# Second expert stage of a two-layer transformer kernel: gates on the inner values, sums kept in PSUM, output matmuls one chunk later

## The chip, the cores and the metric

The kernel runs on one core of a Trainium2 chip. A core has five engines that run on their own and meet through semaphores: TensorE (PE, matmuls), VectorE (DVE), ScalarE (ACT), GpSimd (POOL) and SyncE (SP, which here only issues transfers). PSUM has eight banks of 128 x 512 fp32 values; TensorE writes there, VectorE and ScalarE read. The metric is the device time of one execution in microseconds (us); lower is better.

## The reference, cut to what matters

Two layers, each an attention-like part and an expert part, on 8 x 256 tokens of width 128. Only the expert part of the second layer concerns the change:

```python
def _L1_ffn_ref(hidden_states, Wg, W1, W3, W2):
    B, S, D, F, E, K = (4, 256, 128, 256, 8, 2)
    x = hidden_states.reshape(-1, d)
    gates = jax.nn.softmax(x @ Wg, axis=-1)
    top_g, top_i = jax.lax.top_k(gates, K)
    top_g = top_g / top_g.sum(axis=-1, keepdims=True)
    w = jnp.zeros((t, e), x.dtype).at[jnp.arange(t)[:, None], top_i].add(top_g)
    gate_h = jax.nn.silu(jnp.einsum('td,edf->etf', x, W1))
    up = jnp.einsum('td,edf->etf', x, W3)
    y = jnp.einsum('etf,efd->etd', gate_h * up, W2)
    out = jnp.einsum('te,etd->td', w, y)
    ...
    x = x + gb * _L1_ffn_ref(h, ...)
```

All eight experts are computed for all tokens; the gate w is zero for six of the eight. Since w depends on token and expert alone, it may multiply y or the inner values gate_h * up: the sum is the same but for rounding.

## The kernel before, in words

Everything is held transposed: 128 channels on the partitions, the 2048 tokens along the free axis, in four blocks of 512. The second expert stage goes through 32 steps m = 4 e + t (expert e, token block t). Each step has two chunks c of 128 inner values.

Matmuls are made nearly exact in fp32 by splitting both sides into an upper part (fp32r) and the rest: `three` issues three matmuls, upper by upper, lower weights by upper, upper by lower values. In the profile these are L1055, L1056 and L1057.

For chunk c of step m:

- `hidden1(m, c)` on TensorE: six matmuls into banks c and 2 + c (the W1 and the W3 product), weights from WH and WL, values from HH and HL. It waits until the same chunk of step m - 1 has been read by ScalarE (`act`) and VectorE (`prod`).
- silu on ScalarE, bank c to SG (L587).
- product on VectorE, bank 2 + c times SG, into G (L1025).
- copy on ScalarE, G to its upper part GH (L591).
- subtraction on VectorE, G - GH into GL (L1032).
- `output1(m, c)` on TensorE: three matmuls from GH and GL into bank 4 + t; the two chunks are summed there.

After both chunks `moe_scale` on VectorE (L702) multiplies the bank by the gates WB of the expert and block into YW, and GpSimd adds YW to ACC in SBUF (L297). It is done two steps behind. At the end `residual_acc` (L634) adds ACC, scaled, to X, and SyncE stores X.

TensorE issues `hidden1(m + 1, 0)`, `output1(m, 0)`, `hidden1(m + 1, 1)`, `output1(m, 1)`. The order on each engine is as written; there is no planner. Steps 8 to 23 of TensorE, 8 to 31 of ScalarE are rolled into loops of eight.

Weights: SyncE loads expert e into WS (L224), and GpSimd splits it into WH and WL (L274, L277), in one of two slots. Gates: the routing result CT is stored to memory (L217) and read back, one row spread over all 128 partitions, into one of two slots of WB (L220 for experts 0 and 1, L226 for the rest). L226 waits for `ymul`, the count of finished gate multiplications, and L224 stands behind it in SyncE's queue.

## Time and profile before

| | |
|---|---|
| median of 3 runs | 723.02 us (719.28, 723.02, 723.96) |
| profiled execution | 722.03 us, span 720.2 us |
| TensorE busy | 626.7 us (87%) |
| VectorE busy | 557.3 us (77%) |
| ScalarE busy | 481.3 us (67%) |
| GpSimd busy | 241.2 us (33%) |
| granted TensorE clock, mean | 0.934 |

The span goes from the first to the last instruction on the chip. Busy shares are means over stages that have different limits; the second expert stage takes the last 165 us or so of the span. The granted clock is given as a share of 2.4 GHz. A matmul's end is modelled, so that matmuls overlap in the list: the pace is read from the distance of their starts.

### The profile page before, as it was taken

What the parts mean: (1) busy time and instruction counts of PE and PEld (TensorE: products, weight loads), DVE (VectorE), ACT (ScalarE), POOL (GpSimd) and SP (SyncE); (2) the same over time, 40 slices, a digit from 0 to 9 for tenths busy, and PEclk for the clock granted to TensorE, in tenths of its full rate; (3) what the DMA queues carried; (4) which work ended last, traced back from release to release, by engine and by line L of the source; (5) the groups of instructions that cost most, each with busy time, mean ns of one, the idle gap of its engine ahead of it and who ended that gap; (6) DMA issues with size and microseconds to landing.
All of it is one profiled execution on the core that took longest, in us unless ns stands there. A gap on an engine that the chain in (4) does not pass through costs nothing.

```text
span 720.2 us, 11276 instructions
## 1 busy us (share of the span) xinstructions
PE 626.7 (87%) x3252; PEld 434.0 (60%) x3252; DVE 557.3 (77%) x1308; ACT 481.3 (67%) x843; POOL 241.2 (33%) x192
## 2 busy tenths in 40 slices
PE   7799999998996999999999995846997988999983
PEld 4355555555444578888888882332755765666662
DVE  3647888888866478988888877559897788888887
ACT  5548999999545489999999993585452544444441
POOL 4222222222213133554444533201422233444423
PEclk9789999999996999999999998775997999999996
DMA  6000000000000402211222200000000322111111
GB/s 226 1 0 3 1 2 1 0 0 0 30 1 0 151 1 88 89 44 44 87 88 87 80 0 22 1 0 0 1 0 6 137 81 78 64 63 63 59 54 59
DMA packets 6795, 30.88 MB, mean 43 GB/s; under 512 B 906, under 2 KB 1043, under 8 KB 4435
## 3 DMA queue, kind: packets, MB, share of 16 engines
q1 hardware_dynamic: 6756, 30.42, 11.7%
q8 instruction: 17, 0.28, 0.2%
q14 instruction: 22, 0.18, 0.1%
HBM read 29.23 MB, written 1.19 MB: 42 GB/s over the span
## 4 chain that ended last, share of the span: by engine, by line
PE 55%; DVE 22%; issue 11%; ACT 10%; DMA 1%; POOL 1%; DVEq 1%; ACTq 0%; SPq 0%; POOLq 0%
PE PS L1055 10%; PE PS L1057 10%; PE PS L1056 10%; DVE AR L1025 6%; DVE STAT L747 5%; ACT RA L591 4%; PE PS L1170 3%; PE PS L1132 3%; PE PS L1152 2%; PE PS L1166 2%; PE PS L1197 2%; PE PS L1131 2%; PE PS L1068 2%; PE PS L1077 2%; DVE HN L615 1%
## 5 line engine op out<-in xcount | busy, mean ns | idle before, releaser
L297 POOL TENSOR_TENSOR AR<-AR 128x512 f32<-128x512 f32 x68 | 101.1, 1487 | 227.9 <-DVE AR L702 227.4
L879 DVE TENSOR_TENSOR RA<-AR,RA 128x512 fp32r<-128x512 f32 x140 | 135.8, 996 | 29.2 <-ACT RA L496 28.4
L495 ACT ACTIVATE AR<-PS,BI 128x512 f32<-128x512 f32 x144 | 99.5, 691 | 24.0 <-PE PS L1057 14.1
L1055 PE MATMUL PS<-HH,WH 128*128 128x512 f32 x272 | 108.7, 400 | 1.5 <-DVE AR L1025 1.5
L1056 PE MATMUL PS<-HH,WL 128*128 128x512 f32 x272 | 107.8, 396 | 0.0
L1057 PE MATMUL PS<-HL,WH 128*128 128x512 f32 x272 | 107.7, 396 | 0.0
L1055 PE MATMUL PS<-RA,WH 128*128 128x512 f32 x208 | 86.9, 418 | 17.9 <-DVE RA L1032 17.2
L591 ACT ACTIVATE RA<-AR 128x512 fp32r<-128x512 f32 x64 | 40.5, 632 | 90.0 <-DVE AR L1025 90.0
L496 ACT ACTIVATE RA<-PS,BI 128x512 fp32r<-128x512 f32 x144 | 98.1, 681 | 0.0
L1032 DVE TENSOR_TENSOR RA<-AR,RA 128x512 fp32r<-128x512 f32 x64 | 72.1, 1127 | 27.6 <-ACT RA L591 24.7
L747 DVE CUSTOM_DVE_ANT_0 STAT<-PS,MQ 128x128 f32<-128x128 f32 (+1 forms) x256 | 76.3, 354 | 20.8 <-PE PS L1153 20.3
L1056 PE MATMUL PS<-RA,WL 128*128 128x512 f32 x208 | 82.2, 395 | 0.0
L1057 PE MATMUL PS<-RA,WH 128*128 128x512 f32 x208 | 82.1, 395 | 0.0
L320 POOL TENSOR_TENSOR RA<-QKT,RA 128x512 fp32r<-128x512 f32 x32 | 40.8, 1276 | 122.3 <-ACT RA L423 119.0
L1055 PEld LDWEIGHTS PS<-RA,WH 128*128 128x128 f32 x208 | 39.4, 190 | 40.6 <-DVE RA L1032 28.7
L1055 PEld LDWEIGHTS PS<-HH,WH 128*128 128x128 f32 x272 | 52.1, 191 | 18.8 <-ACT RA L496 3.0
L1057 PEld LDWEIGHTS PS<-HL,WH 128*128 128x128 f32 x272 | 52.0, 191 | 11.2
L1056 PEld LDWEIGHTS PS<-HH,WL 128*128 128x128 f32 x272 | 52.1, 192 | 9.6
L431 ACT ACTIVATE AR<-PS 128x768 f32<-128x768 f32 x64 | 48.4, 808 | 8.8 <-PE PS L1170 8.7
L1077 PE MATMUL PS<-STAT,OND 128*128 128x512 f32 x48 | 31.5, 765 | 21.9 <-ACT STAT L374 21.9
L702 DVE TENSOR_TENSOR AR<-PS,AR 128x512 f32<-128x512 f32 x68 | 46.1, 681 | 1.3 <-POOL AR L297 1.3
L421 ACT ACTIVATE QKT<-PS,KEPT,V 128x256 f32<-128x256 f32 x64 | 36.1, 563 | 14.8 <-PE PS L1132 14.8
(181 smaller groups left out, 1176.6 us busy)
## 6 DMA issues: line engine op xcount, KB each, us to landing
AR<-comb SPq DMA_DIRECT2D x17, 1024.0 KB, 4.7
WS<-in_w SPq DMA_DIRECT2D x9, 512.0 KB, 5.4
WS<-in_w SPq DMA_DIRECT2D x8, 384.0 KB, 5.2
M<-in_mats SPq DMA_DIRECT2D x1, 1384.0 KB, 10.5
X<-in_xT SPq DMA_DIRECT2D x4, 256.0 KB, 4.7
out_xT<-X SPq DMA_DIRECT2D x4, 256.0 KB, 2.1
AR<-in_wmod SPq DMA_DIRECT2D x1, 768.0 KB, 7.3
KM<-in_kmats SPq DMA_DIRECT2D x1, 160.0 KB, 7.9
```

The source lines that it names most:

```text
L297: gp.tensor_tensor(out=blk(ACC, t), in0=blk(ACC, t), in1=YW[:, t % 2, :], op=ALU.add)\
L431: act.activation(PR[:, n0 % 2, 2 * h:2 * h + 2, :], PS[:, 2 + 2 * h:4 + 2 * h, 0:384], ACT.Exp, scale=SCALE).then_inc(exp_done, 1)
L495: act.activation(G[:, c, :], PS[:, c, :], ACT.Gelu_apprx_tanh, bias=bias).then_inc(s["act"], 1)
L496: act.activation(GH[:, m0 % 2, c, :], PS[:, c, :], ACT.Gelu_apprx_tanh, bias=bias)\
L591: act.activation(GH[:, m0 % 2, c, :], G[:, c, :], ACT.Copy).then_inc(s1["gh"], 1)
L702: dve.tensor_tensor(out=YW[:, m0 % 2, :], in0=PS[:, 4 + m0 % 4, :], in1=WB[:, slot, t * BLK:(t + 1) * BLK], op=ALU.mult).then_inc(s["ymul" ...
L747: mm = dve.tensor_tensor_reduce(out=MASKED_S[:, q, j, 0:width], in0=PS[:, j, first:first + width], in1=MQ[:, 256 - width:256], scale=-1.0, ...
L879: dve.tensor_tensor(out=GL[:, m0 % 2, c, :], in0=G[:, c, :], in1=f(GH[:, m0 % 2, c, :]), op=ALU.subtract).then_inc(s["lo"], 1)
L1032: dve.tensor_tensor(out=GL[:, m0 % 2, c, :], in0=G[:, c, :], in1=f(GH[:, m0 % 2, c, :]), op=ALU.subtract).then_inc(s1["lo"], 1)
L1055: pe.matmul(out, wh, xh, start=first, stop=False)
L1056: pe.matmul(out, wl, xh, start=False, stop=False)
L1057: return pe.matmul(out, wh, xl, start=False, stop=last)
```

## The change

The gate now multiplies G, between the product and the copy (`weigh1` on VectorE, once per chunk, in place). The outputs of all eight experts then only need adding, and TensorE does this in PSUM: only expert 0's first chunk starts banks 4 to 7 anew. `moe_scale`, YW, ACC and GpSimd's additions fall away in this stage, and the last scaled addition reads PSUM. GpSimd splits only the weights of experts 0 and 1; for the other six ScalarE makes the copy (`upper_weights1`) and VectorE the subtraction (`lower_weights1`). Every output chunk is issued one chunk later. All loops are written out. `ymul` counts two per step in this stage, and SyncE's wait for it is changed to match: it now asks for both chunks of all steps before expert e - 1. The first expert stage is as before.

```diff
--- before.py
+++ after.py
@@ -222,7 +222,7 @@
                 def later(e, slot):
                     sp.wait_ge(s["split"], 2 * e)
                     sp.dma_start(WS[:, 0:width], w[bass.ds(e, 1), :, :].rearrange("a p n -> p (a n)")).then_inc(s["w_in"], 16)
-                    sp.wait_ge(s["ymul"], 4 * e - 4)
+                    sp.wait_ge(s["ymul"], (4 if n == 0 else 8) * (e - 1))
                     sp.dma_start(WB[:, slot, :], comb[bass.ds(e, 1), :].to_broadcast([128, TOK])).then_inc(s[f"wb_in{slot}"], 16)
 
                 with sp.Fori(0, 3) as it:
@@ -354,9 +354,6 @@
                       .then_inc(ph_done, 1)
             for t in range(NBLK):
                 split_hidden(5, HN, t)
-            gp.wait_ge(x_upd, 12)
-            gp.memset(ACC, 0.0).then_inc(moe[1]["acc_init"], 4)
-            experts(1, E1, 768)
 
 
         @block.scalar
@@ -579,22 +576,32 @@
             router_exp(1)
             s1 = moe[1]
 
-            def silus(m, m0):
-                for c in range(2):
-                    act.wait_ge(s1["h"], 2 * m + c + 1)
-                    if m0 >= 1:
-                        act.wait_ge(s1["prod"], 2 * m - 2 + c + 1)
-                    act.activation(SG[:, c, :], PS[:, c, :], ACT.Silu).then_inc(s1["act"], 1)
-                    act.wait_ge(s1["prod"], 2 * m + c + 1)
-                    if m0 >= 2:
-                        act.wait_ge(s1["y"], m - 1)
-                    act.activation(GH[:, m0 % 2, c, :], G[:, c, :], ACT.Copy).then_inc(s1["gh"], 1)
-
-            for m in range(8):
-                silus(m, m)
-            with act.Fori(1, 4) as it:
-                for u in range(8):
-                    silus(8 * it + u, 8 + u)
+            def silu(m, c):
+                act.wait_ge(s1["h"], 2 * m + c + 1)
+                if m >= 1:
+                    act.wait_ge(s1["prod"], 2 * m - 2 + c + 1)
+                act.activation(SG[:, c, :], PS[:, c, :], ACT.Silu).then_inc(s1["act"], 1)
+
+            def upper1(m, c):
+                act.wait_ge(s1["ymul"], 2 * m + c + 1)
+                if m >= 2:
+                    act.wait_ge(s1["y"], m - 1)
+                act.activation(GH[:, m % 2, c, :], G[:, c, :], ACT.Copy).then_inc(s1["gh"], 1)
+
+            def upper_weights1(e):
+                act.wait_ge(s1["w_in"], 16 * (e + 1))
+                act.wait_ge(s1["y"], 4 * e - 4)
+                act.activation(WH[:, e % 2, 0:768], WS[:, 0:768], ACT.Copy).then_inc(s1["split"], 1)
+
+            silu(0, 0)
+            for m in range(4 * E1):
+                silu(m, 1)
+                upper1(m, 0)
+                if m + 1 < 4 * E1:
+                    silu(m + 1, 0)
+                upper1(m, 1)
+                if m % 4 == 1 and 4 <= m < 4 * E1 - 4:
+                    upper_weights1(m // 4 + 1)
 
 
         @block.vector
@@ -1017,35 +1024,53 @@
             routes_in(1, E1)
             s1 = moe[1]
 
-            def middle1(m, m0, meanwhile=None):
-                for c in range(2):
-                    dve.wait_ge(s1["act"], 2 * m + c + 1)
-                    if m0 >= 1:
-                        dve.wait_ge(s1["lo"], 2 * m - 2 + c + 1)
-                    dve.tensor_tensor(out=G[:, c, :], in0=PS[:, 2 + c, :], in1=SG[:, c, :], op=ALU.mult)\
-                       .then_inc(s1["prod"], 1)
-                    if c == 1 and meanwhile:
-                        meanwhile()
-                    dve.wait_ge(s1["gh"], 2 * m + c + 1)
-                    if m0 >= 2:
-                        dve.wait_ge(s1["y"], m - 1)
-                    dve.tensor_tensor(out=GL[:, m0 % 2, c, :], in0=G[:, c, :], in1=f(GH[:, m0 % 2, c, :]),
-                                      op=ALU.subtract).then_inc(s1["lo"], 1)
-
-            for m in range(3):
-                middle1(m, m)
-            for m in range(2, 8):
-                middle1(m + 1, m + 1, lambda: moe_scale(s1, m - 2, m - 2, 0))
-            with dve.Fori(1, 3) as it:
-                for u in range(8):
-                    middle1(8 * it + u + 1, 9 + u,
-                            lambda: moe_scale(s1, 8 * it + u - 2, 6 + u, it - (u < 2)))
-            for m in range(24, 31):
-                middle1(m + 1, m + 1, lambda: moe_scale(s1, m - 2, m - 2, (m - 2) // 8))
-            for m in (29, 30, 31):
-                moe_scale(s1, m, m, 3)
-            for t in range(NBLK):
-                residual_acc(1, s1, E1, t)
+            def product1(m, c):
+                dve.wait_ge(s1["act"], 2 * m + c + 1)
+                if m >= 1:
+                    dve.wait_ge(s1["lo"], 2 * m - 2 + c + 1)
+                dve.tensor_tensor(out=G[:, c, :], in0=PS[:, 2 + c, :], in1=SG[:, c, :], op=ALU.mult)\
+                   .then_inc(s1["prod"], 1)
+
+            def weigh1(m, c):
+                e, t = m // 4, m % 4
+                if t == 0 and c == 0:
+                    dve.wait_ge(s1[f"wb_in{e % 2}"], 16 * (e // 2 + 1))
+                dve.wait_ge(s1["prod"], 2 * m + c + 1)
+                dve.tensor_tensor(out=G[:, c, :], in0=G[:, c, :], in1=WB[:, e % 2, t * BLK:(t + 1) * BLK],
+                                  op=ALU.mult).then_inc(s1["ymul"], 1)
+
+            def lower1(m, c):
+                dve.wait_ge(s1["gh"], 2 * m + c + 1)
+                if m >= 2:
+                    dve.wait_ge(s1["y"], m - 1)
+                dve.tensor_tensor(out=GL[:, m % 2, c, :], in0=G[:, c, :], in1=f(GH[:, m % 2, c, :]),
+                                  op=ALU.subtract).then_inc(s1["lo"], 1)
+
+            def lower_weights1(e):
+                dve.wait_ge(s1["split"], 2 * e + 1)
+                dve.tensor_tensor(out=WL[:, e % 2, 0:768], in0=WS[:, 0:768], in1=f(WH[:, e % 2, 0:768]),
+                                  op=ALU.subtract).then_inc(s1["split"], 1)
+
+            product1(0, 0)
+            weigh1(0, 0)
+            for m in range(4 * E1):
+                product1(m, 1)
+                lower1(m, 0)
+                weigh1(m, 1)
+                if m % 4 == 2 and 4 <= m < 4 * E1 - 4:
+                    lower_weights1(m // 4 + 1)
+                if m + 1 < 4 * E1:
+                    product1(m + 1, 0)
+                lower1(m, 1)
+                if m + 1 < 4 * E1:
+                    weigh1(m + 1, 0)
+            for t in range(NBLK):
+                dve.wait_ge(s1["y"], 4 * E1 - 3 + t)
+                for b in (2 * t, 2 * t + 1):
+                    ins = dve.scalar_tensor_tensor(out=blk(X, b, SEQ), in0=PS[:, 4 + t, (b % 2) * SEQ:(b % 2 + 1) * SEQ],
+                                                   scalar=MG[:, 1, 1, b:b + 1], in1=blk(X, b, SEQ),
+                                                   op0=ALU.mult, op1=ALU.add)
+                ins.then_inc(x_upd, 1)
 
 
         @block.tensor
@@ -1427,9 +1452,11 @@
             router(1, 3)
             s1 = moe[1]
 
-            def hidden1(m, m0, c):
-                slot, t = m0 // 4 % 2, m0 % 4
-                if m0 >= 1:
+            def hidden1(m, c):
+                slot, t = m // 4 % 2, m % 4
+                if t == 0 and c == 0:
+                    pe.wait_ge(s1["split"], 2 * (m // 4) + 2)
+                if m >= 1:
                     pe.wait_ge(s1["act"], 2 * m - 1 + c)
                     pe.wait_ge(s1["prod"], 2 * m - 1 + c)
                 for which in range(2):
@@ -1438,40 +1465,31 @@
                                True, True)
                 mm.then_inc(s1["h"], 1)
 
-            def output1(m, m0, c):
-                slot = m0 // 4 % 2
+            def output1(m, c):
+                e, t = m // 4, m % 4
+                slot = e % 2
                 w = slice(512 + 128 * c, 640 + 128 * c)
                 pe.wait_ge(s1["lo"], 2 * m + c + 1)
-                if c == 0 and m0 >= 4:
-                    pe.wait_ge(s1["ymul"], m - 3)
-                elif c == 0 and m0 >= 2:
-                    pe.wait_ge(s1["ct"], 1 + m0)
-                mm = three(PS[:, 4 + m0 % 4, :], WH[:, slot, w], WL[:, slot, w], GH[:, m0 % 2, c, :],
-                           GL[:, m0 % 2, c, :], c == 0, c == 1)
+                if e == 0 and c == 0 and t >= 2:
+                    pe.wait_ge(s1["ct"], 1 + t)
+                mm = three(PS[:, 4 + t, :], WH[:, slot, w], WL[:, slot, w], GH[:, m % 2, c, :],
+                           GL[:, m % 2, c, :], e == 0 and c == 0, e == E1 - 1 and c == 1)
                 if c == 1:
                     mm.then_inc(s1["y"], 1)
-
-            def step1(m, m0, e_next, ahead=True):
-                if ahead and m0 % 4 == 3:
-                    pe.wait_ge(s1["split"], 2 * e_next + 2)
-                for c in range(2):
-                    if ahead:
-                        hidden1(m + 1, m0 + 1, c)
-                    output1(m, m0, c)
 
             pe.wait_ge(hl_done, 16)
             pe.wait_ge(s1["split"], 2)
             for c in range(2):
-                hidden1(0, 0, c)
+                hidden1(0, c)
             for t in range(NBLK):
                 route_out(1, E1, t)
-            for m in range(8):
-                step1(m, m, m // 4 + 1)
-            with pe.Fori(1, 3) as it:
-                for u in range(8):
-                    step1(8 * it + u, 8 + u, 2 * it + u // 4 + 1)
-            for m in range(24, 32):
-                step1(m, m, m // 4 + 1, ahead=m < 31)
+            for m in range(4 * E1):
+                for c in range(2):
+                    if m + 1 < 4 * E1:
+                        hidden1(m + 1, c)
+                    if m > 0 or c > 0:
+                        output1(m - (c == 0), 1 - c)
+            output1(4 * E1 - 1, 1)
 
 
 def layouts(inputs):
```

How the instructions stand on two engines at the places that matter, in the order of issue; what each waits for is behind it. "AR" holds G, SG, WB and ACC, "RA" holds GH and GL.

VectorE at the start of the stage, before. L692 is the last of the routing, L1025 the product, L1032 the subtraction:

```order
L692 COPY AR<-PS 8x512 [waits moe1_combT] x4
L1025 TENSOR_TENSOR AR<-PS,AR 128x512 [waits moe1_act]
L1032 TENSOR_TENSOR RA<-AR,RA 128x512 [waits moe1_gh]
L1025 TENSOR_TENSOR AR<-PS,AR 128x512 [waits moe1_act]
L1032 TENSOR_TENSOR RA<-AR,RA 128x512 [waits moe1_gh]
L1025 TENSOR_TENSOR AR<-PS,AR 128x512 [waits moe1_lo,moe1_act]
```

and with the change, where L1031 is the product, L1039 the weighing and L1046 the subtraction:

```order
L699 COPY AR<-PS 8x512 [waits moe1_combT] x4
L1031 TENSOR_TENSOR AR<-PS,AR 128x512 [waits moe1_act]
L1039 TENSOR_TENSOR AR<-AR 128x512 [waits moe1_prod,moe1_wb_in0]
L1031 TENSOR_TENSOR AR<-PS,AR 128x512 [waits moe1_act]
L1046 TENSOR_TENSOR RA<-AR,RA 128x512 [waits moe1_gh]
L1039 TENSOR_TENSOR AR<-AR 128x512 [waits moe1_prod]
```

The second instruction of the stage now waits for the first gates (`wb_in0`), and the second product stands behind it.

VectorE in the later steps, before (L702 is `moe_scale`):

```order
L1025 TENSOR_TENSOR AR<-PS,AR 128x512 [waits moe1_lo,moe1_act]
L702 TENSOR_TENSOR AR<-PS,AR 128x512 [waits moe1_acc,moe1_wb_in1,moe1_y]
L1032 TENSOR_TENSOR RA<-AR,RA 128x512 [waits moe1_y,moe1_gh]
L1025 TENSOR_TENSOR AR<-PS,AR 128x512 [waits moe1_lo,moe1_act]
L1032 TENSOR_TENSOR RA<-AR,RA 128x512 [waits moe1_y,moe1_gh]
```

and with the change (L1051 is the subtraction for the weights, once in four steps for six experts):

```order
L1039 TENSOR_TENSOR AR<-AR 128x512 [waits moe1_prod]
L1051 TENSOR_TENSOR WL<-WS,WH 128x768 [waits moe1_split]
L1031 TENSOR_TENSOR AR<-PS,AR 128x512 [waits moe1_lo,moe1_act]
L1046 TENSOR_TENSOR RA<-AR,RA 128x512 [waits moe1_y,moe1_gh]
L1039 TENSOR_TENSOR AR<-AR 128x512 [waits moe1_prod]
```

Between the subtraction of one chunk and that of the next there are now a weighing and a product, and the waits for GpSimd (`acc`) are gone.

TensorE at the end of the stage, with the change. HH is an operand of hidden matmuls, RA of output matmuls:

```order
L1080 MATMUL PS<-HH,WH 128x512
L1081 MATMUL PS<-HH,WL 128x512
L1082 MATMUL PS<-HL,WH 128x512
L1080 MATMUL PS<-RA,WH 128x512 [waits moe1_lo]
L1081 MATMUL PS<-RA,WL 128x512
L1082 MATMUL PS<-RA,WH 128x512
L1080 MATMUL PS<-RA,WH 128x512 [waits moe1_lo]
L1081 MATMUL PS<-RA,WL 128x512
```

Before, the last hidden matmuls were followed by three groups of output matmuls; now there are four, of which the first belongs to step 30, chunk 0.

## Rows read from the trace of the kernel before

**Rows 1.** Stretches by window: length, busy time (instructions) of each engine, granted clock, DMA share, GB/s.

```profile
543.90:547.00 3.10, 3.10 (x8) 2.45 (x8) 2.40 (x9) 1.75 (x3) 0.94 (x1) 0.50 0.00 0
557.60:704.57 146.97, 132.80 (x547) 98.53 (x545) 121.15 (x149) 67.93 (x122) 57.55 (x40) 1.00 0.20 74
704.57:720.20 15.63, 4.15 (x9) 2.04 (x9) 11.09 (x17) 1.75 (x3) 5.15 (x5) 0.59 0.18 68
```

**Rows 2.** Groups of instructions, 557.6 to 704.57: busy, mean ns | idle before, releaser.

```profile
L1032 DVE TENSOR_TENSOR RA<-AR,RA 128x512 fp32r<-128x512 f32 x61 | 69.0, 1130 | 26.1 <-ACT RA L591 23.3
...
L1025 DVE TENSOR_TENSOR AR<-PS,AR 128x512 f32<-128x512 f32 x60 | 40.9, 681 | 0.0
L297 POOL TENSOR_TENSOR AR<-AR 128x512 f32<-128x512 f32 x28 | 39.7, 1420 | 101.7 <-DVE AR L702 101.7
L591 ACT ACTIVATE RA<-AR 128x512 fp32r<-128x512 f32 x61 | 38.6, 633 | 79.2 <-DVE AR L1025 79.2
L587 ACT ACTIVATE AR<-PS 128x512 f32<-128x512 f32 x61 | 35.4, 580 | 0.0
L1055 PE MATMUL PS<-RA,WH 128*128 128x512 f32 x60 | 26.6, 444 | 14.2 <-DVE RA L1032 13.9
```

**Rows 3.** Timeline before GpSimd adds: start, duration (us), engine, line, operation [idle before].

```profile
561.97 0.69 DVE L1032 TENSOR_TENSOR RA<-AR,RA 128x512 fp32r<-128x512 f32 x1 [0.70 <-ACT RA L591]
...
562.58 0.68 DVE L1025 TENSOR_TENSOR AR<-PS,AR 128x512 f32<-128x512 f32 x1
...
563.30 0.63 ACT L591 ACTIVATE RA<-AR 128x512 fp32r<-128x512 f32 x1 [0.87 <-DVE AR L1025]
...
563.96 0.69 DVE L1032 TENSOR_TENSOR RA<-AR,RA 128x512 fp32r<-128x512 f32 x1 [0.70 <-ACT RA L591]
...
569.15 0.68 DVE L702 TENSOR_TENSOR AR<-PS,AR 128x512 f32<-128x512 f32 x1
```

**Rows 4.** Timeline of TensorE, the same matmul of two successive steps.

```profile
561.70 0.39 PE L1055 MATMUL PS<-HH,WH 128*128 128x512 f32 x1
...
565.78 0.39 PE L1055 MATMUL PS<-HH,WH 128*128 128x512 f32 x1
```

**Rows 5.** Timeline in the middle of the stage, GpSimd and VectorE.

```profile
606.98 1.29 POOL L297 TENSOR_TENSOR AR<-AR 128x512 f32<-128x512 f32 x1 [3.82 <-DVE AR L702]
607.00 1.82 DVE L1032 TENSOR_TENSOR RA<-AR,RA 128x512 fp32r<-128x512 f32 x1
```

**Rows 6.** The list of line L1032, all its instructions.

```profile
L1032 DVE TENSOR_TENSOR RA<-AR,RA x64: 691/694/1878, 556.0 to 708.5; 128x512 fp32r<-128x512 f32 x64
```

**Rows 7.** Timeline of the stage's start; SPq is SyncE's queue.

```profile
554.63 0.67 DVE L1025 TENSOR_TENSOR AR<-PS,AR 128x512 f32<-128x512 f32 x1
...
555.44 0.47 PE L1055 MATMUL PS<-HH,WH 128*128 128x512 f32 x1 [1.46 <-DVE AR L1025]
...
557.18 0.82 SPq L220 DMA_DIRECT2D AR<-comb  x2
...
557.60 0.39 PE L1055 MATMUL PS<-HH,WH 128*128 128x512 f32 x1
```

**Rows 8.** The list of line L220, its two transfers at 557.2 and 557.6.

```profile
DMA to landing us min/median/max: 4.7/5.7/6.8
```

**Rows 9.** The page, DMA issues: KB each, us from issue to landing.

```profile
WS<-in_w SPq DMA_DIRECT2D x8, 384.0 KB, 5.2
```

**Rows 10.** Timeline of the stage's end.

```profile
704.18 0.39 PE L1057 MATMUL PS<-HL,WH 128*128 128x512 f32 x1
...
710.35 0.79 PE L1055 MATMUL PS<-RA,WH 128*128 128x512 f32 x1 [1.55 <-DVE RA L1032]
...
711.37 0.63 PE L1057 MATMUL PS<-RA,WH 128*128 128x512 f32 x1
...
713.36 4.35 DVE L634 SCALAR_TENSOR_TENSOR X<-AR,MG,X 128x256 f32<-128x256 f32 x8
```

**Rows 11.** Timeline, an earlier pair of scaled additions.

```profile
529.27 0.88 DVE L992 SCALAR_TENSOR_TENSOR X<-XC,MG,X 128x256 f32<-128x256 f32 x2
```

## The prediction, made before the changed kernel was timed

> **What bounds the kernel now.** Only the second expert stage is changed, so I first read where it lies and how fast it runs, in the stretches by window [rows 1]. Its body is the stretch of 146.97 us from the first matmul of `hidden1(1, 1)`, 557.60 [rows 7], to the end of `hidden1(31, 1)`, 704.57 (last start 704.18 [rows 10] plus 0.39). TensorE is granted its full 2.4 GHz in it (clock 1.00), is busy for 132.80 us and idle for 14.2: it is nearly the bound, but not quite. The stage has 32 steps m (8 experts by 4 blocks) of 18 matmuls, 576 in all; 21 lie ahead of the stretch and 9 behind it in the present order, so 546 lie in it, or 30.33 steps: **4.85 us a step**.
>
> The groups of instructions [rows 2] tell who holds it back. TensorE's idle time stands before the output matmuls (`L1055` with right operand RA) and is put down to VectorE's subtraction `L1032`. ScalarE is idle for 79.2 us, all of it for VectorE's product `L1025`. VectorE's own idle time is 26.1 us. And `L1032` has a mean of 1130 ns where the product of the same size has 681. The list of that one line [rows 6] shows that the mean hides two prices: minimum 691, median 694, maximum 1878 ns. Before GpSimd begins to add, each takes 0.69 and the next VectorE instruction starts 0.61 behind it [rows 3]. Later the high price stands where GpSimd's addition `L297` runs: GpSimd starts at 606.98, `L1032` at 607.00, and it takes 1.82 [rows 5]. The difference, 1.13 us, is VectorE blocked.
>
> What is the pace without GpSimd? The same matmul of two successive steps starts at 561.70 and at 565.78 [rows 4]: **4.08 us**, 18 matmuls at 0.2267, which is TensorE back to back. So the present order already runs at TensorE's own pace for as long as GpSimd is silent.
>
> **The change, part by part.** I reckon against the profiled execution, 722.03 us, which is 0.99 under the median of 723.02.
>
> *1. The body.* GpSimd's additions and weight splits go, and the 1.82 us subtractions with them. A step's VectorE work becomes two products (0.68), two weighings (SBUF by SBUF like `L1032`, so 0.69; nearest row) and two subtractions (0.69). Six at the distance of 0.61 are 3.66 us, under 4.08. Then there is the chain through two engines: weighing, ScalarE's copy, subtraction, next weighing. [rows 3] time its present counterpart: subtraction 561.97, product 562.58, copy 563.30, next subtraction 563.96, which is 1.99 for half a step, 3.98 for one. The weighing takes the product's place in it (0.69 for 0.68), and the product moves into the 0.7 us in which VectorE waited for ScalarE. So this chain too stays just under 4.08. The lag of one more chunk takes the output matmuls off it: `output1(m, 0)` now comes 9 matmuls (2.0 us) later. TensorE is then the bound. In the new order 18 matmuls lie ahead of `hidden1(1, 1)` and 12 behind `hidden1(31, 1)`, again 546 between: 546 x 0.2267 = 123.8, and 0.2 for the last one's end, 124.0. Against 146.97 this is **-23.0**.
>
> *2. The weight splits.* For six experts ScalarE gets a 128x768 copy and VectorE a 128x768 subtraction; by width at most 0.633 x 1.5 = 0.95 and 0.69 x 1.5 = 1.04 [rows 2, 3]. The copy has ScalarE's idle time as cover (its own work is 2 x 0.58 + 2 x 0.63 = 2.4 us in 4.08). The subtraction has only 0.1 us, so the chain slips by 0.7 to 0.9 each time and wins back 4.08 - 3.98 = 0.1 a step, 0.4 before the next. The slip is free while the product is in time for its banks: 4.08 less 1.53 (six hidden matmuls), less 1.34 (silu and product with their signals), less 0.14 (signal to TensorE, 555.30 to 555.44 [rows 7]) leaves 1.07. Six slips of 0.7 less five recoveries of 0.4 are 2.2, less 1.07: **+1.1**, ends 0 and 2.5.
>
> *3. The start.* Here the change costs. The gates of expert 0, spread over all partitions, are first used at 569.15 [rows 3]; the new order wants them behind the very first product. Their transfer is issued at 557.18 [rows 7] and lands 4.7 us later [rows 8], at 561.9, and nothing ahead of it is altered. VectorE works in order: behind the waiting weighing stands the second product, and behind that product TensorE's `hidden1(1, 1)`. Weighing 561.9, product 562.5 to 563.2, TensorE 563.3 where it is 557.60 now: **+5.7**, ends 5 and 8 (if the gates land as late as the second transfer of the pair, 6.8).
>
> *4. The clock.* TensorE then stands idle from 557.0 to 563.3. Shortly before the stage, after a stretch of small matmuls and gaps, the granted clock is 0.50, which is 1.2 GHz, and stays there through 3.1 us of busy matmuls, 543.90 to 547.00 [rows 1]. At 1.2 GHz half the work gets done, so a like stretch costs **+1.5**, ends 0 (it doesn't fall) and 3.4 (twice as long, with the loop restarting in pieces). The Trainium skill (TensorE: Matmul & The Clock Gate, What's actually happening) speaks against the change here: by it the throttled state is the default and only activity releases it. By that rule the lower end of 0 is to be struck out and the sum stays.
>
> *5. The end.* From the last hidden matmul to the end it is 15.63 us now [rows 1]: the last steps go subtraction, scaling, GpSimd's addition, then come eight scaled additions in 4.35 us from 713.36 [rows 10] and the last store, 720.2 - 717.7 = 2.5. In the new order, from the end of `hidden1(31, 1)`: silu to 0.6, product to 1.3, subtraction and weighing to 2.6, copy to 3.2, last subtraction to 3.9, three matmuls at the low clock as now (710.35 to 712.00 [rows 10]) to 5.7. Meanwhile VectorE does six scaled additions, 0.88 a pair [rows 11] with 0.1 of overlap, 3.9 to 6.3; the last pair to 7.1; the store 2.5: 9.6. That is **-6.0**, ends -4 and -7.
>
> *6. What costs nothing.* GpSimd's memset of the sum and its signal: no other engine waits on them any more. SyncE: the gates of expert e are released when expert e - 2 is weighed, four steps (16 us) ahead of use, and weights are sent for three steps (12 us) ahead of their copy; they land in 4.7 and 5.2 us [rows 8, 9]. If these covers were gone, each expert would stop once for what is missing.
>
> Sum: -23.0 + 1.1 + 5.7 + 1.5 - 6.0 = **-20.7**, so 701.3 by the profiled execution and 702.3 by the median. I say 702. With the ends: 723.02 - 23.0 + 0 + 5 + 0 - 7 = 698, and 723.02 - 23.0 + 2.5 + 8 + 3.4 - 4 = 710.
>
> **Rivals.**
>
> *VectorE and ScalarE become the bound (0.14).* The distance of 0.61 holds only if what an instruction waits for is long done. If each of the six waits for its predecessor's end and 0.04 more (as the copy does behind the product, 563.26 to 563.30), a step is 2 x 0.68 + 4 x 0.69 + 6 x 0.04 = 4.36, with a quarter of 1.04 for the weights 4.6; 0.5 more a step, 16 us: 718, within 1%. For it: only one instruction stands between dependent ones in the new order. Against: in [rows 3] the product follows at 0.61 although it waits on semaphores. A case half way, 4.35, gives 710. The Trainium skill (Advanced Engine Details and Errata, The Read-Write Bubble) says that memory latency is exposed as a bubble between VectorE instructions; by the rows that bubble is inside the 0.61, by this rival it comes on top.
>
> *The subtraction is long for another reason (0.04).* This one ends on the other side. If work from SBUF by SBUF has its mean of 1.13 us [rows 2] whatever GpSimd does, the change doubles such instructions, from two to four a step: 2 x 0.68 + 4 x 1.13 + 0.24 = 6.1, and 30.33 x (6.1 - 4.85) = 38 us, with start, clock and end (+1.2) 762. It decides from a mean of 0.80: (4.81 - 1.36 - 0.24) / 4. For it: transfers into SBUF run in this stage as well. Against: subtractions took 0.69 while the first gates were landing, and the long one starts within 20 ns of a GpSimd row [rows 3, 5].
>
> *The clock stays low after the start (0.04).* The restarted loop might feed TensorE too little to raise it. At 0.43 a matmul a step takes 7.7 us, 3.6 more; five steps are 18, less the 1.5 counted: 719, within 1%. Against: 3.1 us sufficed in [rows 1].
>
> **How the numbers follow.** My own case has 0.78 and gives 702, with 698 to 710. Measurements of this kernel can't tell less than about 1%, 7 us, from no change. The range **697 to 711** takes in my case and the half-way one; the full chain rival, the slow one and the low clock lie outside, with what my case has beyond its ends some 0.2. Faster by over 1% (below 715.8): 0.78 and 0.09 for the half-way case, 0.87. Within 1%: 0.05 and 0.04, 0.09. Slower: 0.04.
>
> **What would show it.** Right: subtraction and weighing at 0.69 with no second price; the same matmul one step later at 4.08 to 4.2; the first weighing held up until about 562, TensorE idle behind it and a lower granted clock after; under 10.5 us from the last hidden matmul to the end. Wrong: steps of 4.4 or more with VectorE busy throughout (first rival), subtractions over 0.8 with GpSimd silent (second), a clock of 0.5 beyond 571 (third).

## The result and the profile after

The changed kernel takes 702.23 us (median of four runs, 700.31 to 704.98), the kernel before 723.49 (719.28 to 724.90). The ratio is 0.971 (95% interval 0.968 to 0.975): about 2.9% faster. In later runs beside other kernels it was 703.00, ratio 0.973 (0.970 to 0.975). The profiled execution took 704.98 us, with a span of 703.2.

The part of the program ahead of the stage is the same, yet it ended later in the profile after: the first product starts at 557.48 there, at 554.63 before [rows 7]. In the thirteen profiles of this study that have this part unchanged, the first product starts anywhere from 554.3 to 557.5 us. To leave this out, I compare the **stage**: from the start of its first product to the end of the span. It fell from 165.6 to 145.7 us, by 19.9. Inside it I name three parts: the *start*, from the first product to the first matmul of `hidden1(1, 1)`, then the *body*, to the end of `hidden1(31, 1)`, then the *end*.

The groups of instructions of the new body, 565.7 to 693.1 (line engine operation, count | busy us, mean ns | idle before, and what ended it), which answer to [rows 2]:

```profile
L1046 DVE TENSOR_TENSOR RA<-AR,RA 128x512 fp32r<-128x512 f32 x62 | 42.7, 689 | 4.3
L1031 DVE TENSOR_TENSOR AR<-PS,AR 128x512 f32<-128x512 f32 x61 | 41.8, 685 | 2.7 <-ACT AR L583 1.5
L1039 DVE TENSOR_TENSOR AR<-AR 128x512 f32<-128x512 f32 x61 | 41.7, 684 | 0.0
L589 ACT ACTIVATE RA<-AR 128x512 fp32r<-128x512 f32 x61 | 38.6, 632 | 30.7 <-DVE AR L1039 30.1
L583 ACT ACTIVATE AR<-PS 128x512 f32<-128x512 f32 x61 | 36.4, 597 | 19.0 <-PE PS L1082 17.6
L1080 PE MATMUL PS<-RA,WH 128*128 128x512 f32 x61 | 24.0, 393 | 0.0
```

The product is L1031 now, the weighing L1039, the subtraction L1046, the copy L589, the silu L583. The subtraction costs 689 ns where it cost 1130; the weighing 684. TensorE waits for no subtraction any more in this stretch (it did for 13.9 us), and ScalarE waits 30.1 us for VectorE where it waited 79.2. The list of L1046 answers to [rows 6]: one price is left.

```profile
L1046 DVE TENSOR_TENSOR RA<-AR,RA x64: 678/692/693, 565.6 to 696.8; 128x512 fp32r<-128x512 f32 x64
```

The stretches by window, as [rows 1]:

```profile
559.90:564.20 4.30, 0.03 (x1) 0.00 (x0) 0.00 (x0) 0.00 (x0) 0.00 (x0) 0.92 0.76 316
564.20:570.30 6.10, 4.60 (x11) 3.71 (x12) 5.52 (x9) 2.86 (x5) 0.00 (x0) 0.50 0.46 185
570.30:693.08 122.78, 122.71 (x538) 100.37 (x537) 116.25 (x184) 75.27 (x124) 0.00 (x0) 1.00 0.19 68
565.70:693.08 127.38, 127.31 (x547) 104.04 (x548) 120.42 (x190) 77.42 (x128) 0.00 (x0) 0.98 0.19 70
693.08:703.20 10.12, 3.42 (x12) 1.66 (x11) 6.78 (x14) 1.86 (x3) 0.00 (x0) 0.84 0.28 104
```

Once the clock is up TensorE shows no idle time, 122.71 of 122.78 us, and outside four short stalls (run 8) its matmuls start 0.2267 us apart: it is the bound. The start has what was feared of it, in the timeline of VectorE, ScalarE, SyncE's queue (SPq) and TensorE:

```profile
557.48 0.67 DVE L1031 TENSOR_TENSOR AR<-PS,AR 128x512 f32<-128x512 f32 x1
...
560.03 0.82 SPq L220 DMA_DIRECT2D AR<-comb  x2
...
564.26 0.69 DVE L1039 TENSOR_TENSOR AR<-AR 128x512 f32<-128x512 f32 x1 [6.11 <-DMA AR<-comb]
564.87 0.68 DVE L1031 TENSOR_TENSOR AR<-PS,AR 128x512 f32<-128x512 f32 x1
...
565.70 0.77 PE L1080 MATMUL PS<-HH,WH 128*128 128x512 f32 x1 [5.77 <-DVE AR L1031]
...
570.68 0.39 PE L1080 MATMUL PS<-HH,WH 128*128 128x512 f32 x1
```

The first weighing waits 6.11 us for the gates, the second product stands behind it, and TensorE behind that.

### The profile page after: what moved, and what is told of

Read it like the earlier page. It is cut to its first block, busy times and chain, and to the rows that moved or that the text cites. A ratio compares the mean times of both kernels' runs of the same rounds, so it can differ in the third digit from the quotient of the medians.

```text
span 703.2 us, 11008 instructions
## 1 busy us (share of the span) xinstructions
PE 623.8 (89%) x3252; PEld 440.1 (63%) x3252; DVE 552.0 (79%) x1346; ACT 491.1 (70%) x849; POOL 176.6 (25%) x147
## 3 DMA queue, kind: packets, MB, share of 16 engines
HBM read 29.23 MB, written 1.19 MB: 43 GB/s over the span
## 4 chain that ended last, share of the span: by engine, by line
PE 73%; DVE 17%; ACT 5%; issue 3%; DMA 2%; POOL 0%; DVEq 0%; SPq 0%; ACTq 0%; POOLq 0%
PE PS L1080 16%; PE PS L1082 16%; PE PS L1081 16%; DVE STAT L754 5%; PE PS L1195 3%; PE PS L1157 3%; PE PS L1177 3%; PE PS L1093 2%; PE PS L1191 2%; PE PS L1156 2%; PE PS L1222 2%; PE PS L1102 2%; PE PS L1231 2%; DVE HN L622 1%; DVE AR L1039 1%
## 5 line engine op out<-in xcount | busy, mean ns | idle before, releaser
L886 DVE TENSOR_TENSOR RA<-AR,RA 128x512 fp32r<-128x512 f32 x140 | 135.8, 995 | 29.2 <-ACT RA L493 28.4
L297 POOL TENSOR_TENSOR AR<-AR 128x512 f32<-128x512 f32 x36 | 56.4, 1566 | 120.8 <-DVE AR L709 120.5
L1080 PE MATMUL PS<-RA,WH 128*128 128x512 f32 x208 | 83.3, 401 | 2.5 <-DVE RA L1046 2.0
L1082 PE MATMUL PS<-RA,WH 128*128 128x512 f32 x208 | 81.7, 393 | 0.0
L589 ACT ACTIVATE RA<-AR 128x512 fp32r<-128x512 f32 x64 | 40.5, 632 | 45.7 <-DVE AR L1039 45.1
L583 ACT ACTIVATE AR<-PS 128x512 f32<-128x512 f32 x64 | 38.2, 597 | 20.4 <-PE PS L1082 19.1
L1039 DVE TENSOR_TENSOR AR<-AR 128x512 f32<-128x512 f32 x64 | 43.8, 684 | 6.1 <-DMA AR<-comb 6.1
L1046 DVE TENSOR_TENSOR RA<-AR,RA 128x512 fp32r<-128x512 f32 x64 | 44.1, 689 | 5.1 <-ACT RA L589 0.7
```

The costliest lines, as they stand in the source:

```text
L297: gp.tensor_tensor(out=blk(ACC, t), in0=blk(ACC, t), in1=YW[:, t % 2, :], op=ALU.add)\
L886: dve.tensor_tensor(out=GL[:, m0 % 2, c, :], in0=G[:, c, :], in1=f(GH[:, m0 % 2, c, :]), op=ALU.subtract).then_inc(s["lo"], 1)
L1039: dve.tensor_tensor(out=G[:, c, :], in0=G[:, c, :], in1=WB[:, e % 2, t * BLK:(t + 1) * BLK], op=ALU.mult).then_inc(s1["ymul"], 1)
L1046: dve.tensor_tensor(out=GL[:, m % 2, c, :], in0=G[:, c, :], in1=f(GH[:, m % 2, c, :]), op=ALU.subtract).then_inc(s1["lo"], 1)
L1080: pe.matmul(out, wh, xh, start=first, stop=False)
L1082: return pe.matmul(out, wh, xl, start=False, stop=last)
```

## The experiments

`ratio` is always to the kernel before, with its 95% interval. The changed kernel stands at 0.971 to 0.973.

**1. Only the additions taken from GpSimd** (`e1_tiny_adds`): does the gain need the gates on the inner values at all?

```diff
-gp.tensor_tensor(out=blk(ACC, t), in0=blk(ACC, t), in1=YW[:, t % 2, :], op=ALU.add)
+gp.tensor_tensor(out=ACC[:, at], in0=ACC[:, at], in1=YW[:, t % 2, 0:wide], op=ALU.add)   # wide = 1
```

> The kernel before, with GpSimd's additions of the second stage cut from 512 columns to 1 (most of the expert sum is left out); gates, PSUM use and order as before. If the gain of the change came from GpSimd no longer blocking VectorE's subtractions, the long subtractions beside the additions go, a step falls from 4.85 to about 4.1-4.2 us, six weight splits on GpSimd still cost 1 to 1.4 us each, and the end loses some 4 us of additions: 704 us, between 700 and 710. If it came from moving the gates and summing in PSUM (less work, another order), nothing of that is touched here and only the end gets shorter: 717 to 723 us.

Measured: 700.29 us, ratio 0.967 (0.966 to 0.969), with a stage of 143.6 us (start 3.0, body 129.7, end 10.9) against 145.7 (8.2, 127.4, 10.1) in the changed kernel. It leaves out most of the work of the expert sum, so its time can't be set beside the changed kernel's as equal work. What it shows is that the pace needs neither the gates on the inner values nor the new order: with GpSimd's additions gone, the old order runs TensorE back to back between the weight splits. Where its six weight splits remain, the long subtraction does too. GpSimd (L277) and VectorE (L1034, the subtraction) of this kernel:

```profile
629.10 1.84 POOL L277 TENSOR_TENSOR WL<-WS,WH 128x768 fp32r<-128x768 f32 x1
```

```profile
627.48 0.69 DVE L1034 TENSOR_TENSOR RA<-AR,RA 128x512 fp32r<-128x512 f32 x1
...
629.51 1.97 DVE L1034 TENSOR_TENSOR RA<-AR,RA 128x512 fp32r<-128x512 f32 x1 [0.70 <-ACT RA L593]
```

**2. and 3. GpSimd put back to work beside the changed kernel**, once reading SBUF, once only writing it. Nobody waits for it in either. Each is one profiled run.

```diff
+for m in range(4 * E1):
+    gp.wait_ge(s1["ymul"], 2 * m + 1)
+    gp.wait_ge(s1["acc"], m + 1)
+    gp.tensor_tensor(out=blk(ACC, m % 4), in0=blk(ACC, m % 4), in1=blk(ACC, (m + 1) % 4), op=ALU.add)   # 2
+    gp.memset(ACC[:, 0:3 * BLK], 0.0)                                                                   # 3
```

> The changed kernel with 32 additions of 128x512 put back on GpSimd, one per step, SBUF by SBUF into scratch that nobody reads or waits for. Blocking: GpSimd starts with the end of the first weighing of a step and takes 1.29 us, so the subtraction that could start 0.7 us later is held 0.6 us or more; a step goes from 4.08 to 4.6 and the weight splits are no longer absorbed: about 720 us (715 to 735). No blocking: 702 us.

> As the last, but GpSimd writes only: 32 memsets of 128x1536, with the same start and about the same length. If what blocks is that both engines read SBUF, the subtractions keep 0.69 us and the time is that of the changed kernel, 702 us. If any work of GpSimd blocks VectorE, it is like the last, about 720 us.

Measured: 719.95 us with the additions, 702.82 with the memsets. The lists of the subtraction, first beside additions (line 1054 of that kernel), then beside memsets (line 1053):

```profile
L1054 DVE TENSOR_TENSOR RA<-AR,RA x64: 674/948/1234, 565.2 to 711.8; 128x512 fp32r<-128x512 f32 x64
```

```profile
L1053 DVE TENSOR_TENSOR RA<-AR,RA x64: 678/692/695, 563.5 to 694.7; 128x512 fp32r<-128x512 f32 x64
```

Minimum, median and maximum are 674, 948 and 1234 ns beside additions, and 678, 692 and 695 beside memsets that keep GpSimd just as long (1.38 us each, 44.3 in all, against 1.30 and 41.5). So GpSimd's writing does no harm; reading does. The two times are single runs, but they lie 17 us apart where the runs of one kernel differ by up to 6. In the timeline the subtraction starts 0.62 us into GpSimd's addition and ends about 0.5 late:

```profile
601.34 1.30 POOL L363 TENSOR_TENSOR AR<-AR 128x512 f32<-128x512 f32 x1 [3.22 <-DVE AR L1047]
...
601.96 1.22 DVE L1054 TENSOR_TENSOR RA<-AR,RA 128x512 fp32r<-128x512 f32 x1
```

The Trainium skill (SBUF — State Buffer, Who interferes with whom) says exactly this: a VectorE instruction with two SBUF inputs contends with a GpSimd instruction that reads SBUF, not with one that only writes it. The two runs agree, 948 against 692 ns in the median.

**4. The changed kernel without the lag of the output matmuls** (`e4_no_lag`).

```diff
-                    if m > 0 or c > 0:
-                        output1(m - (c == 0), 1 - c)
-            output1(4 * E1 - 1, 1)
+                    output1(m, c)
```

> The changed kernel with the output matmuls where they were before (output of a chunk right behind the hidden matmuls of the next step's same chunk). From the start of the hidden matmuls of a chunk to the end of its last subtraction it is about 5.6 us; the output matmuls now want it 4.08 + 1.36 = 5.44 us after, so a step becomes 4.25 and each weight split is paid in full (0.7 to 0.9 for six): 5 to 10 us more than the changed kernel, 707 to 712. If the chain has more room than I think the lag is worth nothing: 702.

Measured: 714.12 us, ratio 0.986 (0.984 to 0.988), 11 to 12 us more than the changed kernel. The direction was right, the size too small. By parts it is 10.9 for the start (8.2 in the changed kernel), 135.6 for the body (127.4) and 9.6 for the end (10.1). The start I had overlooked: without the lag `output1(0, 0)` stands ahead of `hidden1(1, 1)` and waits for the first subtraction, which stands behind the gates. In the body a step took 4.36 us, not 4.25, while a weight split cost 0.4 to 0.6, less than the 0.7 to 0.9 expected. Part of what is missing in the step shows where TensorE resumes. Four starts of it, the second being the output matmul that waited:

```profile
584.91 0.39 PE L1082 MATMUL PS<-HL,WH 128*128 128x512 f32 x1
585.24 0.50 PE L1080 MATMUL PS<-RA,WH 128*128 128x512 f32 x1
585.57 0.40 PE L1081 MATMUL PS<-RA,WL 128*128 128x512 f32 x1
...
589.25 0.39 PE L1082 MATMUL PS<-HL,WH 128*128 128x512 f32 x1
```

The matmul behind the one that waited starts 0.33 us later, not 0.227. So the wait of 0.1 us cost another 0.1. Added to 4.25 that would be 4.35; that the one explains the other is argued, no run separates it. From 584.91 to the same matmul of the next step, 589.25, it is 4.34.

**5. The weight splits back on GpSimd** (`e5_gp_splits`).

```diff
+for e in range(2, E1):
+    gp.wait_ge(moe[1]["w_in"], 16 * (e + 1))
+    gp.wait_ge(moe[1]["y"], 4 * e - 4)
+    split_weights(1, e, e % 2, 768)
```
(and `upper_weights1`, `lower_weights1` not called)

> The changed kernel with the six later weight splits back on GpSimd (as before the change). ScalarE and VectorE lose 5 and 5.7 us of work, but GpSimd's 128x768 subtraction (about 2 us, two SBUF inputs) blocks VectorE's SBUF by SBUF work, which is now four instructions a step. Blocking: each split slips the chain by 1 to 1.8 us instead of 0.7, 0.4 is won back between two, 1.1 is absorbed once: 2 to 5 us more than the changed kernel, 704 to 707. If GpSimd's part in the splits was harmless, the four stalls of 0.25 us that the trace of the changed kernel shows go, and it is 1 us less: 701.

Measured: 710.46 us, ratio 0.982 (0.979 to 0.984), 7 to 8 us more than the changed kernel; I had said 2 to 5. The weighing is now the instruction that gets caught. At each of the six splits one weighing takes 2.32 to 2.34 us beside GpSimd's 128x768 subtraction, and TensorE then waits 0.95 to 1.01 us for five of the six experts. At the first split it is 0.45. The second split, GpSimd and VectorE:

```profile
602.20 2.31 POOL L277 TENSOR_TENSOR WL<-WS,WH 128x768 fp32r<-128x768 f32 x1
```

```profile
602.72 2.33 DVE L1041 TENSOR_TENSOR AR<-AR 128x512 f32<-128x512 f32 x1
```

So a split costs the chain 1.64 us (2.33 for 0.69), inside the 1 to 1.8 expected. Only at the first split is a second instruction long, the subtraction just ahead:

```profile
584.27 0.94 DVE L1048 TENSOR_TENSOR RA<-AR,RA 128x512 fp32r<-128x512 f32 x1
585.13 2.33 DVE L1041 TENSOR_TENSOR AR<-AR 128x512 f32<-128x512 f32 x1
```

With 1.64 the expectation's own sum is 6 x 1.64 - 5 x 0.4 - 1.1 = 6.7, or 5.6 more than the 1.1 of the changed kernel, and the stage is 6.2 longer. The mechanism held, and the 2 to 5 was too low for its own upper slips.

**6. The first gates without the trip through memory** (`e6_pe_gates`). TensorE spreads the row of expert 0 over the partitions, ScalarE copies it to WB.

```diff
+pe.matmul(PS[:, 4 + t, :], IDF[0:8, 0:1].to_broadcast([8, 128]), CT[0:8, t * BLK:(t + 1) * BLK],
+          start=True, stop=True)
...
+act.activation(WB[:, 0, t * BLK:(t + 1) * BLK], PS[:, 4 + t, :], ACT.Copy)
```

> The changed kernel, with the gates of expert 0 spread over the partitions by four matmuls into banks 4 to 7 and four ScalarE copies to SBUF, in place of the transfer through memory. Theory: the 6.1 us that VectorE waits for the first gates and the low clock behind it (2.2 us) are the whole cost of the start. The first weighing comes about 1 us behind the first product instead of 6.8 behind it, the clock stays up: 6 to 8 us less than the changed kernel, 695 us (693 to 697). Rival: the start only moves a wait, since the later gates and weights then come late, or the clock falls anyway after the routing: 699 to 702.

Measured: 697.39 us, ratio 0.963 (0.961 to 0.966), 5 to 6 us less than the changed kernel, a little under the 6 to 8 expected. The stage is 140.2 us instead of 145.7. TensorE's `hidden1(1, 1)` starts 4.7 us behind the first product instead of 8.2, which is 3.5 of the gain, and no slow clock follows (granted clock 1.00 from 556 to 570), which makes the body 2.0 shorter. It is not back at 3.0, since two of the four spreading matmuls (L1499, 1.98 us) lie right ahead of it:

```profile
557.87 0.69 DVE L1049 TENSOR_TENSOR AR<-AR 128x512 f32<-128x512 f32 x1 [0.40 <-ACT AR L598]
...
559.58 1.98 PE L1499 MATMUL PS<-AR,IDF 8*128 8x512 f32 x4
...
561.49 0.50 PE L1090 MATMUL PS<-HH,WH 128*128 128x512 f32 x1
```

**7. GpSimd out of the stage, everything else as before** (`e7_no_gp_old_order`).

```diff
+add1(m - 3)      # VectorE, behind product 0:  ACC += YW
+scale1(m - 2)    # VectorE, behind product 1:  YW = bank * gates
 ...
+upper_weights1(m // 4 + 1)    # ScalarE, at m % 4 == 1
+lower_weights1(m // 4 + 1)    # VectorE, at m % 4 == 2
```

> GpSimd out of the stage by itself: the kernel before, with its order (gates on the outputs, no lag), but the additions to ACC on VectorE and the six weight splits on ScalarE and VectorE. VectorE has the six instructions a step of the changed kernel. Theory: what paid is GpSimd's silence; the gates on the inner values and the lag cost 5.3 us at the start and some clock and gain nothing for the pace. So: first hidden matmuls 3.0 us behind the first product (8.2 in the changed kernel), body 124 to 125 us, end 11.4 (10.1): the stage takes 138.5 instead of 145.7, 695 us (693 to 698). Rival: VectorE's additions in the chain make it the bound, or the splits are not absorbed in this order: a step of 4.3 or more, 702 us or more.

Measured: 703.14 us, ratio 0.971 (0.969 to 0.973), the same as the changed kernel. This was a clear miss, and it changed my picture of what the new order is for. The start was as said (3.0), but the body took 130.3 us and the end 12.0. TensorE is held up twice per expert, by 0.25 and then by 0.7 (at the first split by 0.7 alone). The timeline of the first split shows how: ScalarE's split (L582) stands ahead of the silu, VectorE waits 0.53 for that, and a step on VectorE's split (L1061) finds no room left before TensorE needs the product:

```profile
578.94 0.83 ACT L582 ACTIVATE WH<-WS 128x768 fp32r<-128x768 f32 x1
...
579.68 0.58 ACT L589 ACTIVATE AR<-PS 128x512 f32<-128x512 f32 x1
...
580.29 0.69 DVE L1026 TENSOR_TENSOR AR<-PS,AR 128x512 f32<-128x512 f32 x1 [0.53 <-ACT AR L589]
...
584.28 0.95 DVE L1061 TENSOR_TENSOR WL<-WS,WH 128x768 fp32r<-128x768 f32 x1
...
585.98 0.47 PE L1091 MATMUL PS<-HH,WH 128*128 128x512 f32 x1 [0.42 <-DVE AR L1026]
```

**8. The changed kernel without its six later splits** (`e8_no_splits`, one profiled run).

```diff
-upper_weights1(m // 4 + 1)
+act.wait_ge(s1["w_in"], 16 * (m // 4 + 2))
+act.activation(SU[:, 0, 0:1], SU[:, 0, 1:2], ACT.Copy).then_inc(s1["split"], 2)    # one column
-lower_weights1(m // 4 + 1)
-pe.wait_ge(s1["split"], 2 * (m // 4) + 2)
```

> The changed kernel with the weight splits of experts 2 to 7 left out (their outputs use old weights). If the splits are what makes TensorE late, the four stalls of 0.25 us at every fourth step go, and the body between the low clock and the last hidden matmuls is TensorE back to back, 0.2267 a matmul: 1 us less than the changed kernel. If they come from elsewhere (the new expert's gates, its first matmuls), they stay.

Measured: 702.0 us as a time, where one run can't show 1 us. Its trace can: no two matmuls of the body, from where the clock is up to the last hidden ones, start more than 0.27 us apart. In the changed kernel there are four places where they do, at 627, 644, 661 and 677, once per expert. The body is 126.0 us long, where the changed kernel has 127.4 (127.2 in run 9). The edit also takes out TensorE's wait for the split, but it is not that: in the changed kernel TensorE resumes at 627.29, 0.15 behind the end of the product that starts at 626.46. The stall:

```profile
626.46 0.68 DVE L1031 TENSOR_TENSOR AR<-PS,AR 128x512 f32<-128x512 f32 x1
...
626.90 0.39 PE L1082 MATMUL PS<-RA,WH 128*128 128x512 f32 x1
627.29 0.47 PE L1080 MATMUL PS<-HH,WH 128*128 128x512 f32 x1
627.60 0.39 PE L1081 MATMUL PS<-HH,WL 128*128 128x512 f32 x1
```

**9. The changed kernel again**, beside the runs of 7 and 8.

> The changed kernel once more, on the chip and beside the runs of the last two, so that they can be compared with it directly: 702 us, 0.971 of the kernel before; stage of 145.7 us from the first product to the end, start 8.2, four stalls of 0.25 in the body.

Measured: 703.00 us, ratio 0.973 (0.970 to 0.975); stage 146.1, the four stalls at the same places of the program (0.24 to 0.28 us each, with what the next matmul loses). The start was 8.9, not 8.2: the gates landed 4.9 us after their issue, where it was 4.2 in the first profile.

**10. and 11. The new order, but gates on the outputs** (`e10_outputs_order`), and the same without the lag (`e11_outputs_no_lag`).

```diff
 product1(m, 1)
 lower1(m, 0)
-weigh1(m, 1)
+scale1(m - 2)
 ...
 product1(m + 1, 0)
 lower1(m, 1)
-weigh1(m + 1, 0)
+add1(m - 2)
```
(ScalarE's copy waits for the product instead of the weighing, each expert starts banks 4 to 7 anew, and the last scaled additions read ACC)

> The order of the changed kernel (silu one chunk ahead of the copy, VectorE's product between two subtractions, output matmuls one chunk later, GpSimd out), but the gates on the outputs: VectorE scales each output bank and adds to ACC in SBUF, still six instructions a step. Theory after the run with the old order: that one lost 7 us in the weight splits (each slips the chain product, copy, subtraction by 1.4 us and nothing absorbs it), and 3.0 at the start against 8.2 were its gain. With this order no weighing stands in the chain, the splits are absorbed by a step's 0.4 us of free VectorE time: start 3.0, body 124, end 11.4, a stage of 138.4 us instead of 145.7: 695 us (693 to 698), 0.961 of the kernel before. Rival: the scaling waits for output matmuls that come a chunk later, and VectorE blocks behind it: 702 or more.

> The same without the lag of the output matmuls. If what made the lag worth 12 us was the weighing in the chain, it is now worth nothing: 695 us. If it was ScalarE's order (the copy of a chunk stands behind the silu of the next one, which waits for its hidden matmuls, so the subtraction ends 5.5 us behind the start of the hidden matmuls and is wanted at 5.44), a step is again 4.25 to 4.36: 701 to 706 us.

Measured: 696.32 us, ratio 0.964 (0.962 to 0.966), for the first, and 706.31, ratio 0.978 (0.975 to 0.981), for the second. The first has a stage of 138.2 us (138.4 expected): start 2.3, body 123.9, end 12.0. In its whole body no two matmuls start more than 0.27 us apart. Its groups from 559 to 682:

```profile
L1031 DVE TENSOR_TENSOR AR<-PS,AR 128x512 f32<-128x512 f32 x61 | 42.0, 688 | 10.0 <-ACT AR L583 6.3
L1067 DVE TENSOR_TENSOR RA<-AR,RA 128x512 fp32r<-128x512 f32 x61 | 41.5, 680 | 0.0
...
L1102 PE MATMUL PS<-RA,WH 128*128 128x512 f32 x60 | 23.3, 389 | 0.0
```

The second shows that the lag is needed for the new order, not for the weighing: without it a step is 4.37 us although nothing is weighed, where the old order without lag (run 7) has 4.08 in its plain steps. Its trace shows what the output matmul (598.36) waits for, ScalarE's silu and copy first, then VectorE's product and subtraction, then TensorE:

```profile
596.38 0.60 ACT L583 ACTIVATE AR<-PS 128x512 f32<-128x512 f32 x1 [1.17 <-PE PS L1104]
...
596.88 0.62 ACT L589 ACTIVATE RA<-AR 128x512 fp32r<-128x512 f32 x1
...
597.01 0.69 DVE L1031 TENSOR_TENSOR AR<-PS,AR 128x512 f32<-128x512 f32 x1 [0.40 <-ACT AR L583]
...
597.62 0.68 DVE L1067 TENSOR_TENSOR RA<-AR,RA 128x512 fp32r<-128x512 f32 x1
...
598.36 0.50 PE L1102 MATMUL PS<-RA,WH 128*128 128x512 f32 x1
```

Both the copy and the subtraction of a chunk stand behind work on the next one, which waits for its hidden matmuls: the copy behind its silu on ScalarE, the subtraction behind its product on VectorE. The subtraction follows the product at the usual 0.61, and the copy had ended 0.12 earlier. So it is the order on both engines, not ScalarE's alone as I had put it; no run changes only one of them.

Runs 6 and 10 are both faster than the kernel before and the changed one. They can't be told apart (0.961 to 0.966 against 0.962 to 0.966).

## Why the prediction was right, point by point

The forecast was 702 us and the measured median 702.23. That they meet within 0.3 us is partly luck: the medians lie 21.3 us apart, the stages of the two profiles 19.9 and the profiled executions 17.0, because the part ahead of the stage ends up to 3 us earlier or later. What can be tested is the stage, term by term:

| step of the prediction | said | measured |
|---|---|---|
| 1. body at TensorE's pace | -23.0 | -22.9: 127.4 us less the 1.0 and 2.3 of the rows below, for 147.0 |
| 2. weight splits | +1.1 | +1.0: four stalls of about 0.25 |
| 3. start | +5.7 | +5.25: 8.22 behind the first product for 2.97 |
| 4. clock | +1.5 | +2.3: 12 matmuls in 4.98 us for 2.72 |
| 5. end | -6.0 | -5.5: 10.13 for 15.63 |
| sum | -20.7 | -19.9 |

*The body.* Once the clock was up TensorE ran at 0.2267 a matmul. VectorE's weighings start 0.59 to 0.61 behind the subtraction ahead, as read from the quiet stretch of the kernel before, and have a median of 684 ns. The subtraction starts 0.78 behind the product, since it waits for the copy. With the product 0.60 behind the weighing a chunk takes 1.99, which is the chain of 3.98 a step that the prediction had read. So the first rival, that each instruction waits for its predecessor's end, did not come. The second rival, that the subtraction is long for another reason, fell with runs 2 and 3. The third, a clock that stays low, did not come either: it was up at 570.3.

*The splits.* The accounting of slack was right in its mechanism too. In plain steps the product starts 1.06 us behind the last hidden matmul of its chunk, and ScalarE's copy of the weights leaves it there. VectorE's first weight subtraction puts it at 1.70; it wins back to 1.19, the second puts it at 2.00, and back to 1.47. That is slips of 0.6 to 0.8 (said: 0.7), 0.5 won back (said: 0.4), and TensorE late from about 2.06, a slack of 1.0 (said: 1.07). The first two of six cost TensorE nothing, the other four 0.25 each; worked out, 0.3.

*The start* was a little cheaper because the gates landed in 4.2 us, not 4.7; in run 9 it was 4.9, so this is spread and no property of the change. *The clock* was dearer. It fell during the idle time (a mean of 0.92 up to 564.2), was 0.50 until 570.3, and so stayed low through 4.6 us of matmuls where the row that I took it from had 3.1. I had put 3.4 as the far end of the cost, so this was inside. By the Trainium skill (TensorE: Matmul & The Clock Gate, What's actually happening) the throttled state is the default and activity releases it. The traces agree with that and not with my lower bound of 0: the clock fell while TensorE stood idle for 5.77 us, and in run 6, where the spreading matmuls kept it busy, it was 1.00 throughout. *The end* took 0.5 more, because the last subtraction ended 4.4 us behind the last hidden matmul, not 3.9. The prediction also had the last three matmuls at the low clock as before; they started 0.34 and 0.23 apart, the high level, but VectorE's additions were under way by then, so this gained little. Step 6, what costs nothing, held: VectorE waited for gates once, at the start.

What the prediction had not asked is what each part of the change earns. It ascribed the pace to GpSimd's silence, and runs 1 to 3 confirm that. Run 7 takes GpSimd out, hands its work to VectorE and ScalarE, keeps the old order, and has the same ratio as the whole change, 0.971. The new order with its lag then holds the pace through the weight splits (body 123.9 in run 10 against 130.3 in run 7), and the gates on the inner values shorten the end (10.1 against 12.0 in both). But they cost 5.3 us of wait at the start and 2.3 of low clock behind it, as steps 3 and 4 had forecast, and that takes back what the order and the end give. Run 6 wins back 5.5 of it; run 10 avoids it and has a stage 7.5 shorter.

Left open, and not tried: what moves the end of the unchanged part by up to 3 us between profiles, and a kernel that changes the order on only one of ScalarE and VectorE.

## What to carry to other kernels

When an engine's instruction has two prices in one line's list, look for who runs beside the dear ones, before counting anybody's work; a small job that reads SBUF on GpSimd can set the pace of the whole loop through VectorE. A gate that moves from the end of a chain to its start moves its transfer to the start as well: ask when it lands, and what stands behind its first user in the queue. And judge an order by its odd steps (here the weight splits): the old order reached the same pace in plain steps, but lost about 6 us where something extra had to go in.

## What was not expected of the hardware

- Blocking depends on what GpSimd does, not on whether it is busy: 1.38 us of memset beside a subtraction leaves it at 0.69, 1.30 us of addition makes it up to 1.23.
- TensorE pays for each resumption at the high clock: the matmul behind the one that waited starts 0.30 to 0.35 us later where 0.227 is the rule, even when the wait itself was 0.1 us.
